# The last feed-forward of a four-layer kernel: a cap on its scatter's writes, and a product of its final sum moved to ScalarE

## The reference

```python
logits = x_tokens @ router_w + router_b
probs = jax.nn.softmax(logits, axis=-1)
vals, idx = jax.lax.top_k(probs, K)                      # K = 2 of E = 16
vals = vals / (jnp.sum(vals, axis=-1, keepdims=True) + 1e-09)
...
expert_inputs = jnp.zeros((E, C, d), x.dtype).at[idx_flat, pos_c].add(x_pair)
expert_outputs = jax.vmap(_mlp)(expert_inputs, w_gate, w_up, w_down)
gathered = expert_outputs[idx_flat, pos_c] * (vals_flat * within)[:, None]
output_tokens = gathered.reshape(N, K, d).sum(axis=1)
return x + _mlp(x, sw_gate, sw_up, sw_down) + output_tokens.reshape(b, s, d)
```

## Time and profile before

| | |
|---|---|
| median of 3 runs | 3823.2 us (3817.73 to 3826.79) |
| the profiled execution's own time | 3827.29 us |
| its span, first to last instruction | 3825.6 us |
| mean granted TensorE clock | 0.955 |
| PE busy / PE weight loads | 3393.0 us (89%) / 2277.0 us (60%) |
| DVE / ACT / POOL busy | 2417.0 / 1850.3 / 1725.7 us |
| the changed function | from 3524.9 to 3809.2 us of the span |

### The profile page before, as it was taken

How to read it: one execution, slowest core, us unless ns; L and a number is a source line. 1 busy time by engine, 2 the same in 40 slices (tenths; PEclk the granted TensorE clock), 3 DMA queues, 4 the chain that set the end, 5 groups by cost and what they waited for, 6 DMA issues and landing times. The chain is left out here.

```text
span 3825.6 us, 70661 instructions
## 1 busy us (share of the span) xinstructions
PE 3393.0 (89%) x24704; PEld 2277.0 (60%) x24704; DVE 2417.0 (63%) x5419; ACT 1850.3 (48%) x5019; POOL 1725.7 (45%) x1887
## 2 busy tenths in 40 slices
PE   6888888869999989999997999988999999998395
PEld 3555553647777756666663444446777777776274
DVE  4887852556666646666663444457888888887135
ACT  4666665466666634544544000036666666664031
POOL 2555531327777743333330000014677667666543
PEclk8999998979999989999998999988999999999697
DMA  4888840030000000000003767743552222223323
GB/s 132 217 211 211 211 125 10 1 76 1 2 2 2 2 1 2 1 2 2 1 2 80 156 152 149 154 87 95 121 113 79 73 77 78 73 79 89 111 68 99
DMA packets 312552, 300.58 MB, mean 79 GB/s; under 512 B 72137, under 2 KB 227721, under 8 KB 311946
## 3 DMA queue, kind: packets, MB, share of 16 engines
q1 hardware_dynamic: 307594, 286.58, 30.5%
q0 software_dynamic: 4608, 9.48, 0.7%
HBM read 237.45 MB, written 58.53 MB: 77 GB/s over the span
## 5 line engine op out<-in xcount | busy, mean ns | idle before, releaser
L2413 DVE TENSOR_TENSOR_SCAN a_h<-a_dA,a_dBu_psum 128x512 f32<-128x512 f32 x512 | 595.8, 1204 | 117.1 <-issue 106.4
L2298 POOL TENSOR_TENSOR a_h<-a_h,main_g 128x512 f32<-128x512 f32 x256 | 383.9, 1502 | 255.7 <-DVE a_h L2413 245.6
L1246 POOL TENSOR_SCALAR a_probs<-a_probs,a_row_inv 128x128 f32<-128x128 f32 (+1 forms) x512 | 380.0, 763 | 163.9 <-DVE a_row_inv L1209 163.9
L1712 DVE SCALAR_TENSOR_TENSOR m_hidden<-m_h_psum,m_gate_spread 128x512 f32<-128x512 f32 x256 | 176.6, 691 | 263.3 <-PE m_h_psum L1650 249.7
L179 POOL TENSOR_TENSOR main_g<-main_g,main_s 128x512 f32<-128x512 f32 x28 | 44.0, 1604 | 658.7 <-ACT main_g L161 658.7
L1515 POOL TENSOR_TENSOR r_position_q<-r_turned_q 128x512 f32<-128x512 f32 x128 | 159.7, 1269 | 390.9 <-DVE r_turned_q L1560 390.9
L2009 PE MATMUL a_dBu_psum<-a_B_diag,a_dt_u_turned 64*128 64x128 f32 x4096 | 317.1, 289 | 20.6 <-DVE a_h L2413 19.8
L1472 ACT ACTIVATE r_probs<-r_logits_psum,r_neg_max 128x256 f32<-128x256 f32 x512 | 235.0, 475 | 140.8 <-DVE r_neg_max L1566 140.8
L2009 PEld LDWEIGHTS a_dBu_psum<-a_B_diag,a_dt_u_turned 64*128 64x128 f32 x4096 | 257.9, 188 | 74.8 <-issue 70.9
L1151 ACT ACTIVATE a_probs<-a_logits,a_neg_max 128x128 f32<-128x128 f32 (+1 forms) x512 | 226.6, 446 | 127.0 <-DVE a_neg_max L1195 127.0
L2032 PE MATMUL a_y_psum<-main_ident,a_h 128*128 128x128 f32 x2048 | 274.8, 276 | 7.7 <-POOL a_h L2298 6.7
(11 more groups left out here) (522 smaller groups left out, 7629.6 us busy)
## 6 DMA issues: line engine op xcount, KB each, us to landing
m_gate_spread<-m_gate_rows SPq DMA_DIRECT2D x64, 1024.0 KB, 8.4
main_g<-a_b_c_rows SPq DMA_DIRECT2D x256, 256.0 KB, 3.2
a_band_rows<-main_g SPq DMA_DIRECT2D x64, 512.0 KB, 4.1
a_B<-a_band_rows SPq DMA_DIRECT2D x192, 128.0 KB, 3.4
a_A<-a_band_rows SPq DMA_DIRECT2D x192, 128.0 KB, 3.3
f_x_expert<-f_x_rows SPq DMA_DIRECT2D x16, 322.5 KB
f_x_rows<-a_zero SPq DMA_DIRECT2D x16, 320.0 KB, 5.2
f_stage_w<-L_ffn_up_weights SPq DMA_DIRECT2D x9, 512.0 KB, 6.9
```

Source lines behind the costliest of these rows:

```text
L1246: ins = nc.gpsimd.tensor_scalar(pr[:, h % NPR, tile[t]], pr[:, h % NPR, tile[t]], rinv[:, p % NST, q:q + 1], None, ALU.mult)
L2298: tt(h[:, r, :, :], h[:, r, :, :], Cs[:, g % NCS, :, :], ALU.mult).then_inc(hc_pool, 1)
L2413: nc.vector.tensor_tensor_scan(flat, dA[:, M % NDA, q, k, :, :].rearrange("p n t -> p (n t)"), db[:, 2 * (g % 2) + k, :], 0.0, ALU.mult, A ...
```

## The change

Two edits in `l3_ffn`. POOL's writes of the scatter count on three semaphores in turn, one for each token tile of three, and before the writes of token tile n POOL waits until those of token tile n - 3 have landed: at most six writes are on their way. SP waits for all three. In the sum, the product of the first choice moves from DVE to ACT, where it is an activation Copy with the weight as its scale, after ACT's last Silu; ACT waits for the loads of the group and for a free buffer of `acc`, DVE waits for ACT's product (`weighed`), and DVE's product with its `link` go.

```diff
-        NX, NH, NXT, NG = 3, 3, 3, 4
+        NX, NH, NXT, NG, NSENT = 3, 3, 3, 4, 3
...
-        sent = s.sems("sent")
+
+        sent = [s.sems(f"sent{i}") for i in range(NSENT)]
...
+                for n in range(NT):
+                    if n % 4 == 0:
+                        act.wait_ge(y_in[n // 4], 16 * TOPK)
+                    if n >= NG:
+                        act.wait_ge(back_mm, n - NG + 1)
+                    nc.scalar.activation(acc[:, n % NG, :], two[:, n, 0, 0:P], ACT.Copy,
+                                         scale=route.gate[:, n, 0:1]).then_inc(weighed, 1)
...
                 for n in range(NT):
                     pool.wait_ge(rows_in[n // 4], 16 * TOPK)
+                    if n >= NSENT:
+                        pool.wait_ge(sent[n % NSENT], 16 * TOPK * (n // NSENT))
                     for k in range(TOPK):
                         nc.gpsimd.indirect_dma_start(route.x_rows,
                                                      bass.IndirectOffsetOnAxis(ap=route.dest_u[:, n, k:k + 1], axis=0),
-                                                     two[:, n, k, :], None).then_inc(sent, 16)
+                                                     two[:, n, k, :], None).then_inc(sent[n % NSENT], 16)
...
                 def combine(n):
                     dve.wait_ge(y_in[n // 4], 16 * TOPK)
-                    if n >= NG:
-                        dve.wait_ge(back_mm, n - NG + 1)
-                    link(ts(acc[:, n % NG, :], two[:, n, 0, 0:P], route.gate[:, n, 0:1], None, ALU.mult))
+                    dve.wait_ge(weighed, n + 1)
                     stt(out=acc[:, n % NG, :], in0=two[:, n, 1, 0:P], scalar=route.gate[:, n, 1:2], in1=acc[:, n % NG, :],
                         op0=ALU.mult, op1=ALU.add).then_inc(combined, 1)
...
-                sp.wait_ge(sent, 16 * NT * TOPK)
+                for i in range(NSENT):
+                    sp.wait_ge(sent[i], 16 * TOPK * len(range(i, NT, NSENT)))
```

More of the change, by code:

```diff
@@ L2501, in l3_ffn @@
         tr, gp, upp, op = s.banks("turned", 2), s.banks("gate", 2), s.banks("up", 2), s.banks("o", 2)
-        (turn_mm, turn_sb, g_mm, u_mm, silued, hidden, o_mm, o_sb, step, combined, back_mm, added, id_made, id_sb, goal_sb, x_in,
+        (turn_mm, turn_sb, g_mm, u_mm, silued, hidden, o_mm, o_sb, weighed, combined, back_mm, added, id_made, id_sb, goal_sb, x_in,
          shared_in, loaded) = s.sems(
-            "turn_mm turn_sb g_mm u_mm silued hidden o_mm o_sb step combined back_mm added id_made id_sb goal_sb x_in "
+            "turn_mm turn_sb g_mm u_mm silued hidden o_mm o_sb weighed combined back_mm added id_made id_sb goal_sb x_in "
             "shared_in loaded")
@@ L2635, in _ @@
             def _(dve):
-                link = Link(dve, step)
-                tt, ts, stt = nc.vector.tensor_tensor, nc.vector.tensor_scalar, nc.vector.scalar_tensor_tensor
+                tt, stt = nc.vector.tensor_tensor, nc.vector.scalar_tensor_tensor
                 def hide(i):
```

## The result

The changed kernel takes 3804.3 us (median of 8 runs, 3795.3 to 3813.9), beside 3824.1 us for the kernel before (8 runs, 3817.7 to 3826.8): a ratio of 0.9948, 95% interval 0.9938 to 0.9959.

What follows compares the result with a forecast made beforehand. The prediction took the scatter, paced by POOL's issue of writes, to set when experts' rows can be read, and DVE to lag the loads at the end. From 3823.2 us, -7.3 + 1.5 = -5.8 us gave 3817.4 us, range 3808 to 3825 us.

Steps and rivals of the forecast that it cites:

- The sum at the end: End of the feed-forward: with first-choice products on ACT, the last add ends at 3801.9 instead of 3809.17, -7.3 us.
- The cap's hold: Scatter, while tokens and weights load: POOL waits for earlier writes to land, +1.5 us, bounds 0 to 7 us.
- The row that I sized it by: Loads of 256 KB while DMA engines are busy: up to 6.3 us to land, exactly the cap's slack.
- The upper bound: Scatter's loaded phase: writes landing in 9.7 us, half the last weight load's time, would hold it 7 us.
- its fourth rival: The cap holds the whole scatter: at a landing of 8.5 us it takes 104 us, total 3839 us; chance 0.05.
- For the PE stall I take 0: Shared expert under the scatter, DVE and ACT released 11.2 us apart: the cap was to change nothing there, 0 us.
- the cap breaks the stall: Shared expert under the scatter: more chunks get done there, total 3802 to 3787 us; chance 0.10.
- Its lesser form: Relief only in the loaded phase of the scatter: about 6 more shared chunks let through, 16 us.
- full relief: Shared chunks end before 3613 and the experts start about 3617, 30 us earlier.
- the forecast's sum of -5.8 us: Whole kernel: -7.3 us at the end's sum plus 1.5 us of hold in the scatter, giving 3817.4 us.

Runs made afterwards that it cites:

- e6: The cap of six writes alone, DVE's sum as in the kernel before; 3811.6 us, ratio 0.9974 to the kernel before (3821.7 us on that chip).
- e5: The changed kernel once more, with nothing altered, beside the kernel before at 3821.7 us; 3806.2 us, ratio 0.9953.
- e8: The changed kernel, with POOL also waiting for all writes on their way before token tiles 8, 16 and 24; 3801.3 us, ratio 0.9943 to the kernel before.
- e3: The kernel before with its writes counted on three semaphores in turn, without the wait; 3783.1 us, ratio 1.0002 to the kernel before.
- e7: The kernel before with only the product moved to ScalarE, one semaphore and no cap; 3815.4 us, ratio 0.9978 to the kernel before (3821.7 us).

## Why the forecast was wrong

*The sum at the end: right.* Forecast -7.3 us (-7.7 to +0.5), with the last add 3.1 us behind the last load. Measured -7.6 us in the profile and 3.2 us; the runs give -8.4 us (-5.0 to -11.8) on one chip and -5.7 us (-1.5 to -9.5) on another. ACT's product is 390 ns against 0.39 us. The Trainium skill ("ScalarE: Activation LUTs", section "What ACT_TABLE_LOAD costs") has the price from which 386 ns were estimated for it, and the trace agrees to 4 ns; its rule that would keep the multiplication on VectorE ("Rules for kernel authors") did not decide here, as VectorE was the engine in the way.

*The cap's hold: right in kind, too small by 1 to 3 us.* Forecast +1.5 us (0 to 7); the first read came 2.4 us later in the changed kernel, 2.4 and 2.7 us on chips without the stall, and 4.0 and 4.1 us in e6 and e5. From its first write to its last the scatter took 2.6 to 3.4 us more than the 79.8 us of before in all five. Gaps lay only before 3564, as said. The row that I sized it by, a landing of 6.3 us, stood at the lower edge of what the writes that held POOL took (6.4 to 8.6 us). The upper bound was too low by the prediction's own terms: a round of six takes the landing and one step more, as its fourth rival reckons, so a landing of 9.7 us gives 33 x (1 - 7.6 / 11.0) = 10 us and not 7.

*The experts' phase: no change forecast*, and -1.0 us in the profile, inside what it does by itself on such a chip (132.8 to 136.5 us in six profiles).

*"For the PE stall I take 0": this step failed.* It was worth -9.6 us in the profile of the changed kernel, -14.0 us in e5 and -16.4 us in e6 (the turned rows' gain plus the hold: 9.9 + 4.1 and 12.4 + 4.0), and -28.5 us with the full pauses of e8. The argument was that from 3566 to 3612, where releases are furthest apart, only two writes are on their way, so that a cap of six can't change that state. That much is true, and the trace after shows the same far releases from 3588 on. But it looked for the effect where the stall is worst and not where the cap bites. The cap bites before 3564; the stall was already there (10 matmuls in 12 us where chunks at full pace start 57, as e3's 3552 to 3564 has them), and what relieves it is not the number of writes on their way but the pause that the cap happens to make. The two facts stood side by side in the prediction, a hold of 1.5 us in the loaded phase and a stall in the same phase, and the sum did not put them together; only a rival did, without naming the pause.

*The rival that came true* is "the cap breaks the stall", given 0.10. Its lesser form named the place (the loaded phase) and priced it at 16 us for six more chunks; two to five more came through, 7 to 12 us net of the hold. With the 7.6 us of the sum that makes the 15 to 20 us that were measured. That full relief (30 us) stayed away fits a cap that pauses once or twice only.

*And the size depends on the chip.* Where the kernel before takes 3780 to 3786 us there is no stall, the cap costs 2 us, and the forecast's sum of -5.8 us is near what is measured (-5.3 us by the ratio, -0.4 to -10.2). The prediction took the stall for a property of the kernel; it shows where the change was measured and on the chip of e5 to e8, and not on the three chips of the other experiments.

What stays open: what differs between the chips (or the machines that they sit in, or what else ran there), and whether the issuing of indirect writes, their bytes, or any work of POOL is what delays the ends of PE's work. That pauses shorten the delay is shown by the kernels with none, one, two and three of them on one kind of chip; that it is the pause and not what POOL's wait does besides is argued, from the SiLU that comes within 0.6 us of the write behind the second full pause. Nor is a best version shown. Where the stall is, full pauses have the lowest median (3801.3 us against 3806.2 us, with intervals that overlap). Where it isn't, the kernel with them is 5 us slower than the one before (3788.4 us against 3783.1 us), and the product alone (ratio 0.9985) and the changed kernel (0.9986, on another chip) can't be told apart.

## What to carry to other kernels

A stall that the profile shows must be asked two things: where is it, and where does the change touch it; here one pause of 2.35 us ahead of its worst stretch went with 9.6 us less of leftover work. When an engine is released late though the one before it was long done, look at what runs beside the two, not at the releaser's name: here a long unbroken row of indirect writes. And run the kernel before on more than one chip before a gain of half a per cent is put down to a mechanism: by the ratios this change is worth 18 to 20 us on one kind and 5 us on the other, and only the 6 to 8 us of the product are there on both.

## What the runs showed of the hardware

- The same kernel takes 3822 to 3824 us on some chips and 3780 to 3786 us on others (8 and 21 runs against 35, 13, 1 and 1), with no overlap but for the one run at 7053 us, at a granted clock that hardly differs (0.955 in the profile of before, 0.958 in e3). Between these two profiles 43.3 of the 45.0 us lie in the two stretches in which POOL issues indirect writes.
- On the slow kind the ends of matmuls reach the engines that wait for them late during such writes: with no pause a SiLU came 24.5 and then 33.6 us after the one before it (e7), where 2.6 us is the chunk's own pace (e3). The experts' stretch, 121.7 us in e3, is 12.7 us longer in before; its releases were not followed one by one, so that this is the same delay is argued.
- Where the delay occurs, the SiLUs keep their 2.6 us for some 7 us of unbroken writes and come later after that (3559.36 to 3566.63 behind the 7.2 us pause of e8). Pauses of 2.1 us let the overdue end through and about one chunk more, and no full pace follows.
- TensorE pays a second time: while it waits it falls to the lower of its two clock levels (granted 0.50, 1.2 GHz, from 3576 to 3588) and the matmuls that follow run at that: 0.36 us each for the five of that stretch in the profile after, against 0.21 us at 1.00 (57 in e3's 12 us).
- An indirect write costs POOL 0.96 us and a gap of 0.30 us, whether a row has 8 or 516 bytes.
